# Second FFN of a two-layer kernel: all experts' weights kept on chip and tiles of 128 rows as the stationary operand

## The reference, cut to what matters

```python
probs = softmax(xf @ gate)                  # xf: [4096, 256], 4 experts
w, idx = top_k(probs, 2); w = w / sum(w)
comb = einsum('nk,nke->ne', w, one_hot(idx, 4))
for e in range(4):
    h = silu(xf @ w1[e]) * (xf @ w3[e])     # [., 768]
    out = out + comb[:, e:e+1] * (h @ w2[e])
```

## Time and profile before

| | us |
|---|---|
| median of 3 runs | 3434.73 (3430.2 to 3435.3) |
| the profiled execution's own time | 3430.11 |
| its span, first to last instruction | 3428.4 |
| routing, from its first instruction to the expert phase | 2762.5 to 2888.3 |
| expert stage, first to last of its matmuls | 2893.6 to 3390.3 |

### The profile page before, as it was taken

One profiled execution on the slowest core, in us unless ns is written; L12 is line 12 of the kernel. 1 busy time (PEld: TensorE's weight loads), 2 busy tenths in 40 slices (PEclk: granted clock), 3 DMA queues, 4 the chain that ended last, 5 costly groups with the idle time before them and its releaser, 6 DMA issues. The chain is left out here.

```text
span 3428.4 us, 72718 instructions
## 1 busy us (share of the span) xinstructions
PE 3172.3 (93%) x22708; PEld 2368.0 (69%) x22708; DVE 2362.7 (69%) x6854; ACT 2093.3 (61%) x4947; POOL 1190.4 (35%) x1854
## 2 busy tenths in 40 slices
PE   4999999999999999989999969879999955999995
PEld 3776777677667777768888855456666654888884
DVE  5888888888888888866666646456666535666665
ACT  4777777777777777755555543146565621555553
POOL 4444444444444444443333320132422102334432
PEclk9999999999999999999999989979999957999998
DMA  2111111111111111143334331101111034455445
GB/s 87 36 33 34 35 35 35 34 31 30 32 35 35 35 35 35 35 155 125 122 129 135 123 111 50 57 16 28 32 27 32 23 121 150 120 142 130 128 120 166
DMA packets 165548, 246.35 MB, mean 72 GB/s; under 512 B 30770, under 2 KB 115506, under 8 KB 165426
## 3 DMA queue, kind: packets, MB, share of 16 engines
q1 hardware_dynamic: 150834, 224.85, 21.4%
q0 software_dynamic: 14592, 19.93, 3.5%
HBM read 159.79 MB, written 41.16 MB: 59 GB/s over the span
## 5 line engine op out<-in xcount | busy, mean ns | idle before, releaser
L770 POOL TENSOR_SCALAR at_p<-at_p,at_recip 128x512 f32<-128x512 f32 (+3 forms) x1030 | 534.7, 535 | 827.5 <-DVE at_recip L917 827.5
L826 ACT ACTIVATE at_p<-at_p,at_nmax 128x512 f32<-128x512 f32 (+3 forms) x1032 | 570.6, 555 | 131.3 <-DVE at_nmax L911 124.7
L911 DVE CUSTOM_DVE_ANT_0 at_p<-at_s_ps,at_bias 128x512 f32<-128x512 f32 (+3 forms) x1032 | 462.2, 488 | 63.7 <-PE at_s_ps L1043 45.0
L1882 DVE CUSTOM_DVE_ANT_0 aa_a_ps<-aa_a_ps,aa_hidden 128x128 f32<-128x128 f32 (+3 forms) x512 | 247.2, 507 | 173.9 <-PE aa_a_ps L2046 170.9
L1043 PE MATMUL at_s_ps<-at_k_twice,at_q 64*128 64x512 f32 (+3 forms) x3096 | 342.5, 340 | 3.1 <-DVE at_nmax L911 3.1
L1065 PE MATMUL at_o_ps<-at_pT,at_v 128*64 128x512 f32 (+3 forms) x2064 | 306.6, 439 | 0.0
L1782 ACT ACTIVATE aa_pT<-aa_b_ps 128x512 f32<-128x512 f32 (+1 forms) x384 | 196.6, 529 | 176.2 <-PE aa_b_ps L2064 173.3
L923 DVE COPY at_pT<-at_t_ps 128x512 f32<-128x512 f32 (+3 forms) x512 | 239.2, 488 | 93.9 <-PE at_t_ps L1055 90.1
L1055 PEld LDWEIGHTS at_t_ps<-ident,at_p 64*128 64x128 f32 x5120 | 189.2, 138 | 120.5 <-issue 120.5
L526 DVE SCALAR_TENSOR_TENSOR nw_hl<-nw_h,nw_coef_now,nw_hh 128x512 fp32r<-128x512 f32 x192 | 149.8, 780 | 162.6 <-ACT nw_hh L454 162.6
L449 ACT ACTIVATE nw_h<-nw_h_ps,nw_b 128x512 f32<-128x512 f32 x192 | 132.1, 688 | 211.0 <-PE nw_h_ps L553 210.6
(11 more groups left out here) (317 smaller groups left out, 8047.1 us busy)
## 6 DMA issues: line engine op xcount, KB each, us to landing
w_raw<-in_w_dram SPq DMA_DIRECT2D x57, 768.0 KB, 5.9
at_k_twice<-at_k_twice SPq DMA_DIRECT2D x130, 256.0 KB, 2.8
nw_w_raw<-in_w_all_dram SPq DMA_DIRECT2D x26, 1024.0 KB, 5.0
nw_w_raw<-in_w_all_dram SPq DMA_DIRECT2D x52, 512.0 KB, 6.8
nw_xh<-xh_dram SPq DMA_DIRECT2D x10, 512.0 KB, 4.2
nw_xl<-xl_dram SPq DMA_DIRECT2D x10, 512.0 KB, 4.9
at_w_raw<-in_w_heads_dram SPq DMA_DIRECT2D x18, 256.0 KB, 3.8
nw_x<-in_x_dram SPq DMA_DIRECT2D x9, 512.0 KB, 5.9
```

Of the source, the lines that this page charges most:

```text
L770: pool.tensor_scalar(p, p, recip[:, u:u + 1], 1.0, ALU.mult, ALU.mult).then_inc(scaled, 1)
L826: act.activation(p_sb[:, u, 0:N], p_sb[:, u, 0:N], ACT.Exp, bias=nmax[:, u:u + 1], scale=-1.0, accum_out=total[:, u:u + 1]).then_inc(exped, 1)
L911: dve.tensor_tensor_reduce(out=p_sb[:, u, 0:N], in0=s_ps[u % 2][:, score_at(u // 2)], in1=bias[:, u % 2, S - N:S], scale=1.0, scalar=BIG, ...
L1882: dve.tensor_tensor_reduce(out=a_ps[i % 2][:, 0:N], in0=a_ps[i % 2][:, 0:N], in1=hidden[:, S - N:S], scale=1.0, scalar=BIG, op0=ALU.add, o ...
```

## The change

The tile of the expert stage becomes 128 rows (`XS`), which makes 67 tiles, and a unit is half of the hidden features (384). The four experts' weights, high and low, are all held in on-chip memory (`w_all`, 147,456 bytes of each partition, laid over y and other buffers once they are read), so the expert stage neither loads nor splits weights. TensorE reads a tile's expert from `owner` into a register and addresses `w_all` by it. x, 128 rows, is the stationary operand and the weights move, 384 columns; the hidden values come out row-major and TensorE turns them (`turn_hidden`, three transposes a unit) before `output_sums`. ScalarE alone takes the output, one block a tile.

In the routing TensorE turns y itself; g2 is multiplied into the gate, and the reciprocal root is applied to all logits at once. The norms for the stored rows go to ScalarE. The weights are loaded in the routing, experts 2 and 3 first, experts 0 and 1 over y after it has been read; ScalarE makes the high parts, GpSimd the low parts of experts 2 and 3 around its `told`, VectorE those of 0 and 1 at the end. Seven of eight images of y are stored to DRAM in the attention phase.

```diff
+XS = P
+HALF1 = H1 // 2
+M2 = HALF1 // P
+XB = XS // P
+TILES = (CH * T + E1 * (XS - 1)) // XS
+STEPS_E = T // XS
+LANES = TILES * XB
...
 # attention_phase, SP, after spread_out(G)
+                if G % KV1 == KV1 - 1 and G > KV1:
+                    b = G // KV1 - 1
+                    sp.wait_ge(dve_out, out_by(PLACE[b, "out1"]))
+                    sp.dma_start(acc_view[:, b * TT:b * TT + TT, :], y[:, b * TT:b * TT + TT, :]).then_inc(acc_stored, 16)
...
 # routing_phase, SP
+            for e in (2, 3):
+                load_expert(sp, w1, w3, w2, w_all, e, w_loaded[e])
...
+            sp.wait_ge(voted, B)
+            sp.wait_ge(others_stored, 48)
+            for i in range(4):
+                sp.wait_ge(rows_stored[i], 32)
+            for e in (0, 1):
+                load_expert(sp, w1, w3, w2, w_all, e, w_loaded[e])
 # routing_phase, GpSimd
+            def split_low(number, e, piece):
+                hi, lo = (slice(at, at + W_PIECE) for at in W_PIECES[piece])
+                pool.wait_ge(w_high, number + 1)
+                pool.tensor_tensor(w_all[:, e, lo], w_all[:, e, lo].bitcast(F32), w_all[:, e, hi].bitcast(F32), ALU.subtract)\
+                    .then_inc(w_low, 1)
...
+            for number in range(6):
+                split_low(number, *pieces[number])
             for j in range(PARTS):
                 pool.wait_ge(marked, 2 * j + 2)
...                                         (told)
+                if j < PARTS - 1:
+                    for number in (6 + 2 * j, 7 + 2 * j):
+                        split_low(number, *pieces[number])
 # routing_phase, ScalarE
+            for b in range(B):
+                square(b)
+                copy_turned(b)
...
+            for b in range(2):
+                norm(b)
+            act.wait_ge(chain, 4)
             act.activation(prob[:], prob[:], ACT.Exp).then_inc(exped, 1)
+            for b in range(2, B):
+                norm(b)
+            for e in (2, 3, 0, 1):
+                act.wait_ge(w_loaded[e], 48)
+                for hi, lo in W_PIECES:
+                    act.activation(w_all[:, e, hi:hi + W_PIECE], w_all[:, e, lo:lo + W_PIECE].bitcast(F32), ACT.Copy)\
+                        .then_inc(w_high, 1)
 # routing_phase, VectorE, at the end
+            for e in (0, 1):
+                for hi, lo in (tuple(slice(at, at + W_PIECE) for at in piece) for piece in W_PIECES):
+                    number += 1
+                    dve.wait_ge(w_high, number)
+                    dve.tensor_tensor(w_all[:, e, lo], w_all[:, e, lo].bitcast(F32), w_all[:, e, hi].bitcast(F32), ALU.subtract)\
+                        .then_inc(w_low, 1)
 # routing_phase, TensorE
+            turn(0)
             for b in range(B):
                 if b + 1 < B:
+                    turn(b + 1)
...
+                pe.wait_ge(copied_a, b + 1)
+                pe.wait_ge(copied_d, b + 1)
...
 # expert_phase, ScalarE
+            for U in range(UNITS):
+                t, half = divmod(U, 2)
+                if U + 1 < UNITS:
+                    pass_gate(U + 1)
+                if half == 0 and t > 0:
+                    take_out(t - 1)
+                act.wait_ge(h_turned, U + 1)
+                if U >= 2:
+                    act.wait_ge(unit_done, U - 1)
+                act.activation(hh[:, half, :], t_ps[half][:, 0:HALF1], ACT.Copy).then_inc(h_high, 1)
+                if half == 0 and t + 1 < TILES:
+                    take_x(t + 1)
 # expert_phase, VectorE
+            for U in range(UNITS):
+                t, half = divmod(U, 2)
+                if U + 1 < UNITS:
+                    gate(U + 1)
+                dve.wait_ge(h_high, U + 1)
+                dve.tensor_tensor(hl[:, half, :], t_ps[half][:, 0:HALF1], hh[:, half, :].bitcast(F32), ALU.subtract)\
+                    .then_inc(h_low, 1)
+                if half == 0 and t + 1 < TILES:
+                    rest_x(t + 1)
 # expert_phase, TensorE
+            def whose(t):
+                expert[t] = pe.value_load(owner[0:1, t:t + 1], min_val=t // STEPS_E, max_val=E1 - 1)
...
+            def hidden_sums(U):
+                t, half = divmod(U, 2)
+                p, e = t % 2, ds(expert[t], 1)
+                if half == 0:
                     pe.wait_ge(x_low, t * KT + KT)
+                if U >= 2:
+                    pe.wait_ge(gated, U - 1)
+                for c, bank in ((0, a_ps[half]), (1, b_ps[half])):
+                    for i, (w, x) in enumerate([(w13h, xh[p]), (w13l, xh[p]), (w13h, xl[p])]):
                         for k in range(KT):
+                            ins = pe.matmul(bank[:, 0:HALF1], x[:, k, :],
+                                            w[:, e, c, k, half * HALF1:half * HALF1 + HALF1].rearrange("p e h -> p (e h)"),
                                             start=(i == 0 and k == 0), stop=(i == 2 and k == KT - 1))
...
+            def turn_hidden(U):
+                half = U % 2
+                pe.wait_ge(gated, U + 1)
+                if U >= 2:
+                    pe.wait_ge(h_low, U - 1)
+                for m in range(M2):
+                    ins = pe.transpose(t_ps[half][:, P * m:P * m + P], hid[:, half, P * m:P * m + P], ident[:])
+                ins.then_inc(h_turned, 1)
...
+            whose(0)
             turn_x(0)
+            hidden_sums(0)
+            hidden_sums(1)
+            turn_hidden(0)
             for U in range(UNITS):
+                t, half = divmod(U, 2)
+                if half == 0 and t + 1 < TILES:
+                    whose(t + 1)
                     turn_x(t + 1)
                 if U + 2 < UNITS:
+                    hidden_sums(U + 2)
+                if U + 1 < UNITS:
+                    turn_hidden(U + 1)
+                output_sums(U)
```

More of the change, by code:

```diff
@@ L25, with hold @@
 HD = 64
-def hold(ctx, nc, spent=None):
+def hold(ctx, nc, spent=None, side=None):
     def sb(name, shape, dt=F32):
-        return ctx.enter_context(nc.sbuf_tensor(name, shape, dt))
+        return ctx.enter_context(nc.sbuf_tensor(name, shape, dt, side=side))
     def ps(name, shape=(P, 512)):
@@ L2204, in routing_phase @@
         sb, ps, sem = hold(ctx, nc)
+        squares = sb("rt_squares", [P, TT, D])
+        blank = sb("rt_blank", [P, TT, D])
+        yr = [sb(f"rt_yr{i}", [P, TT, D]) for i in range(4)]
+        yT = [[sb(f"rt_yT{i}{k}", [P, S]) for k in range(KT)] for i in range(2)]
+        sb, _, _ = hold(ctx, nc, side="right")
         table = sb("rt_table", [P, TABLE_COLS])
-        squares = sb("rt_squares", [P, TT, D])
-        sq_sum = sb("rt_sq_sum", [P, TT])
-        rms = sb("rt_rms", [P, TT])
-        r2 = sb("rt_r2", [P, 2, TT])
+        sq_sum = sb("rt_sq_sum", [P, NT])
+        rms = sb("rt_rms", [P, NT])
+        r2 = sb("rt_r2", [P, NT])
         eps = sb("rt_eps", [P, 1])
-        blank = sb("rt_blank", [P, TT, D])
-        yr = sb("rt_yr", [P, NT, D])
-        yg = [sb(f"rt_yg{i}", [P, KT, S]) for i in range(2)]
         g2_sb = sb("rt_g2", [P, KT])
@@ L2222, in routing_phase @@
         ends = sb("rt_ends", [P, 6, E1])
-        over = sb("rt_over", [P, E1, B])
+        over = sb("rt_over", [P, E1, STEPS_E])
         late = sb("rt_late", [1, TILES, E1 - 1])
@@ L2235, in routing_phase @@
         y_ps = [[ps(f"rt_y_ps{i}{k}") for k in range(KT)] for i in range(2)]
-        l_ps = [ps(f"rt_l_ps{i}") for i in range(2)]
+        l_ps = ps("rt_l_ps")
         c_ps = ps("rt_c_ps")
@@ L2241, in routing_phase @@
         blanked = sem("rt_blanked")
-        stored = sem("rt_stored")
+        rows_stored = [sem(f"rt_rows_stored{i}") for i in range(4)]
+        others_stored = sem("rt_others_stored")
         squared = sem("rt_squared")
@@ L2574, in _ @@
-            sp.wait_ge(w_low, UNITS)
-            for b in range(4, B):
-                load_sides(b)
+            for e in range(2):
+                sp.wait_ge(unit_done, (e + 1) * STEPS_E * 2)
+                for b in range(e * B // 2, (e + 1) * B // 2):
+                    for to, at in zip(sides(b), (s_view[b], x_view[b])):
+                        sp.dma_start(to, at).then_inc(side_loaded[b], 16)
+            sp.wait_ge(unit_done, UNITS)
             sp.wait_ge(scattered, LANES * 16)
-            for b in range(len(sums)):
-                sp.dma_start(sums[b][:], acc_view[b]).then_inc(acc_loaded[b], 16)
@@ L2623, in take_out, with pass_gate @@
-                for i in range(2):
-                    act.activation(o_sb[t % 2][:, i, :], o_ps[0][:, i * D:i * D + D], ACT.Copy,
-                                   scale=shares[:, t * TT + i:t * TT + i + 1]).then_inc(taken_a, 1)
+                    act.wait_ge(scattered, (t - 1) * 16)
+                act.activation(o_sb[t % 2][:], o_ps[:, 0:D], ACT.Copy, scale=shares[:, t:t + 1]).then_inc(taken, 1)
+            def pass_gate(U):
+                act.wait_ge(ready, U + 1)
+                act.activation(act1[:, U % 2, :], a_ps[U % 2][:, 0:HALF1], ACT.Silu).then_inc(silued, 1)
@@ L2627, in _ @@
             act.wait_ge(g2_loaded, 16)
```

(19 more changed lines are left out.)

352 lines of the change are left out of this document (130 added, 222 removed).

## The result

The kernel after takes 3605.81 us (median of 4 runs, 3599.78 to 3609.46), the kernel before 3432.47 (median of 4 runs, 3430.2 to 3435.3): 1.0504 times, 95% interval 1.0491 to 1.0517. It is slower, by 173 us; 3529 was forecast, with a range to 3615. The profiled execution took 3604.48, its span is 3602.7 against 3428.4.

A forecast was written before the change was run, and what follows sets the result against it. TensorE's own instructions were taken to bound the expert stage. Terms 115.7 - 16.6 + 12 - 4.6 - 3.3 - 5.9 = +97.3 us on 3430.11 gave 3527.4, stated as 3529 us, range 3475 to 3615.

The forecast's parts named there:

- main forecast: Whole kernel: slower through a stall in each expert tile, 3529 us, own bounds 3490 to 3575, chance 0.62.
- the rival of the late gather: Expert stage: a gather or the sequencer sets the tile period, +35 to +70 us, 3565 to 3600; chance 0.14.
- The wait: Expert stage: TensorE idles for the next tile's x, turned right before use, 1.94 us a tile, 130 us in all.
- TensorE's own work: Expert stage: matmuls and transposes of a 128-row tile take 7.20 us, 67 tiles 482.4 us, 14.3 less than now.
- The read into the register: Expert stage: value_load of the tile's expert on TensorE falls in the stall and costs 0.
- Size of the stage: Expert stage: 67 tiles of 9.14 us make 612.4 us against 496.7, +115.7 us.
- The first rival: Expert stage: the clock falls in each stall, 1.5 us a tile, +100 us, 3630; chance 0.13.
- The sign of being wrong: Expert stage: TensorE busy without gaps, or a period set by xg or by a granted clock under 0.9.
- Voting: Routing: TensorE becomes the bound as it turns y itself, 43.1 us against 59.7, -16.6.
- Lists: Routing: GpSimd's twelve low parts cost +13.5 us beside VectorE, shorter lists give back 1.5, sum +12.
- Rest of the routing: End of routing: three gathers in place of twelve, but VectorE has 12 low parts, 13.1 us, -4.6.
- The other side: Expert stage: no stall, x ready at its first matmul, tile 7.20 us, time 3397 us; chance 0.05.

The follow-up runs named there:

- e2: Kernel after with the turn of x (turn_x, take_x, rest_x) one half earlier and 5 buffers of gathered rows in place of 3: 3410.55 us.
- e7: e2 with the expert's number read into the register three times in place of 67, weights still addressed by register: 3410.72 us.
- e11: Kernel after with 5 buffers of gathered rows in place of 3 and nothing else changed: 3605.77 us.
- e5: Kernel after with GpSimd's twelve low parts of the weights given to VectorE, which makes all 24 behind the lists: 3600.64 us.
- e8: Kernel after with the edits of e2 and e5 together: 3401.04 us.
- e10: e8 with both parts of experts 2 and 3 made by VectorE between the images of the voting: 3390.58 us.
- e1: Kernel after with 15 idle matmuls of 256 columns per tile issued behind turn_x, where TensorE waits: 3556.27 us.
- e6: Kernel before with its turn of x moved from step 1 to step 4 of a tile, right ahead of its use: 3494.11 us.
- e3: e2 with 3 buffers of gathered rows in place of 5: 3621.22 us.
- e4: Kernel after with take_x ahead of take_out and hh on ScalarE, rest_x ahead of hl on VectorE, TensorE's order unchanged: 3525.31 us.

## Why the prediction was right, and where it was short

The direction, the place of the loss and its mechanism were right; the size was short. The forecast was +97 us and +173 was measured. That the range held it is luck: the main forecast's own bounds were 3490 to 3575, the range reached 3615 because of the rival of the late gather, which did not come true, and it left out the rival that came true in half of the tiles, the clock.

**The wait** is where the prediction put it, ended by `rest_x`, 1.97 us against 1.94. The working from the start of the stall holds up to `rest_x` within 0.06 (`take_out` at 0.20, `hh` at 0.58, `take_x` at 0.95, `rest_x` at 1.61); then two `rest_x` take 0.61 and not 0.49, and TensorE (its weight load and its matmul within 0.01) starts 0.14 behind VectorE's end and not 0.05. From the slot in which TensorE would go on, 3208.90, to its start at 3211.26 are 2.36 us, 2.16 forecast. A stall thus takes 9.40 - 7.19 = 2.21 us of a tile, more than the 1.97 that shows as idle, where forecast and tile work gave 1.94.

**TensorE's own work** was right: 7.19 by e2 against 7.20, with 0.174 (2.09 / 12) for 384 columns against 0.175. Errors inside cancel: a transpose takes 0.08 (0.24 for three) and not 0.11, but the output matmuls take 1.14 for nine with the change of operand and not 1.06, and in e2 the half behind the turn of x takes 2.20 in place of 2.09.

**The read into the register, the gather**: 0 and in time, as taken (e7, e11). The landing, 5.6 us and more in the earlier trace rows, is 2.8 now (median), so the rival's sum was too dark. The gather is now one behind one scatter, where four gathers stood behind four; that may be why, but no run tests it.

**Size of the stage.** This is the term that failed: 67 x 9.14 = 612.4 was forecast, 684.4 measured. Of the 72 us between them 67 x 0.26 = 17 are the longer stall and 34 x 1.57 = 53 the clock, which the sum had put at nothing. The first rival, that the clock falls in each stall, gave 1.5 us a fall (measured 1.57) and had a chance of 0.13; it came true in half of the tiles. What I held against it, that 1.94 is shorter than the 2.3 us after which the earlier trace rows show a fall, was an argument from a single row that was no lower bound. The result lies between the two cases. The sign of being wrong, a clock under 0.9 in the stage, was set too low to catch it: with falls in half of the tiles it reads 0.91.

**Routing.** Voting -19.2 against -16.6, TensorE the bound as argued (votes 3.27 apart and turns 1.74, both a little under their records). Lists +16.6 against +12: the twelve splits, 21.7 us at their price alone (12 x 1.81), cost VectorE 18.6 by e5, where 13.5 was taken. Rest of the routing -6.0 against -4.6, first x -3.0 against -3.3, end -5.8 against -5.9. The 4.0 us ahead of the voting had no term. 2.9 of them are there before the first new store of y, and the executions of e8 and e10, whose code is the same up to there, differ by 3.7 at this point: most of it can be the scatter of single executions.

**The other side**, 3397 with no stall, is what e2 made of the change: 3410.55. Of the 13 between, 4.0 are the stretch ahead of the voting and some 5 the stage (487 us against 482.4); the rest is spread over the routing, the end and the 0.9 between the profiled execution and the median.

Left open: which of two equal stalls in a row the fall of the clock picks. The runs show only that stalls of 1.45 us alone never had one, stalls of 1.97 to 2.3 had one in about half of the tiles or more, and filled stalls none, nor did the one wait of 2.4 us for rows in e1. Each of these runs changes the length of the stalls and their distance together, so no limit for either can be read from them.

## What to carry to other kernels

When a tile gets smaller, look again at how far ahead each hand-over is made: a turn that passes three engines took 2.4 us with tiles of 128 rows and 3.3 with 512 (e6): it shrinks far less than the tile. It has to be issued that much other work before its use; here one half of a tile was enough (e2), with the gathers moved ahead to match (e3). An idle stretch on TensorE can cost more than its length, since the clock may fall behind it: take it away (e2), shorten it (e4), or fill it (e1), in this order of gain. GpSimd is no free hand for splits while VectorE has work with two on-chip inputs (e5): look for idle time of VectorE itself (e10).

## What the runs showed of the hardware that I had not expected

- The granted clock falls to its half level behind idle stretches of TensorE of 1.97 us in 34 of 66 tiles, behind 2.3 us in 11 of 17, and behind 1.45 us alone in none (e4; both times that a wait of 2.2 to 2.3 us stood right ahead of the 1.45, it fell). Each fall costs 1.57 us, in both kernels. Fifteen matmuls a tile whose result nobody reads are worth 50 us (e1).
- A VectorE step of 0.29 us with two on-chip inputs takes 1.8 us beside a GpSimd subtraction of 768 columns; a reduction of one input, 0.38 us, is untouched.
- A gather of 128 rows lands 2.8 us (median) after its issue in the kernel after, behind one scatter, and 5.6 to 7.5 in the kernel before, where four gathers stand behind four scatters.
- Reading a register from on-chip memory on TensorE once per tile costs nothing that 64 reads would show (3410.72 against 3410.55 us).
